# Routing of a token group in nine items instead of four, with the fourth group placed after the attention

## The reference

```python
x = x + _L2_xattn_ref(_layernorm(x, axis=-1), ctx_1024, ...)
def _L2_ffn_ref(x, ...):
    x = x + attention(layernorm(x, ln1_w), c_attn_w, c_proj_w)      # causal, 16 heads
    x = x + moe_mlp(layernorm(x, ln2_w), router_w, w1, w2)
def moe_mlp(x, router_w, w1, w2):
    probs = jax.nn.softmax(router_logits.astype(jnp.float32), axis=-1)
    rw, sel = jax.lax.top_k(probs, K)                               # K = 2 of E = 8
    h = jax.nn.gelu(jnp.einsum('nc,ecf->enf', xf, w1e), approximate=False)
    y = (y_sel * rw[:, :, None]).sum(axis=1)
```

## Time and profile before

| | |
|---|---|
| median of 3 runs | 3309.73 us (3307.66 to 3317.76) |
| profiled execution, its own time | 3314.98 us |
| its span | 3313.2 us |
| busy: PE, DVE, ACT, POOL | 85%, 60%, 50%, 34% of the span |
| granted TensorE clock, mean | 0.921 of full speed |

### The profile page before, as it was taken

How to read it: one execution, slowest core, us unless ns; L and a number is a source line. 1 busy time by engine, 2 the same in 40 slices (tenths; PEclk the granted TensorE clock), 3 DMA queues, 4 the chain that set the end, 5 groups by cost and what they waited for, 6 DMA issues and landing times. The chain is left out here.

```text
span 3313.2 us, 69870 instructions
## 1 busy us (share of the span) xinstructions
PE 2813.2 (85%) x25966; PEld 1896.0 (57%) x26085; DVE 1984.3 (60%) x4625; ACT 1663.2 (50%) x3058; POOL 1137.0 (34%) x1192
## 2 busy tenths in 40 slices
PE   4999686888789999999969999998469958999993
PEld 2554463555346666666635556666269936676672
DVE  4887555888455433433358887787554345555547
ACT  2778342777444444444427776766355513333332
POOL 6653008887000000000043334464400064565513
PEclk8999896999779999999969999999789968999995
DMA  3332002222214000000011211111243233332301
GB/s 115 74 74 60 14 5 90 66 67 68 45 53 147 1 1 1 1 1 1 1 60 58 74 47 51 41 61 56 81 143 97 84 100 79 81 83 63 77 20 51
DMA packets 164743, 189.87 MB, mean 57 GB/s; under 512 B 25968, under 2 KB 136832, under 8 KB 164256
## 3 DMA queue, kind: packets, MB, share of 16 engines
q1 hardware_dynamic: 147520, 143.44, 14.5%
q0 software_dynamic: 16896, 41.97, 4.9%
HBM read 67.09 MB, written 41.42 MB: 33 GB/s over the span
## 5 line engine op out<-in xcount | busy, mean ns | idle before, releaser
L1900 DVE TENSOR_TENSOR f1H<-f1HF,f1H 128x512 bf16<-128x512 f32 x256 | 176.6, 692 | 398.3 <-ACT f1H L1740 398.3
L1695 PE MATMUL ps<-f1w,f1H 128*128 128x256 bf16 x3072 | 379.1, 274 | 0.0
L1673 PE MATMUL ps<-f1xT,f1w 128*128 128x512 bf16 x1448 | 360.3, 384 | 12.1 <-ACT f1H L1740 5.9
L1695 PEld LDWEIGHTS ps<-f1w,f1H 128*128 128x128 bf16 x3072 | 301.8, 98 | 90.8 <-issue 1.7
L1737 ACT ACTIVATE f1HF<-ps 128x512 f32<-128x512 f32 x256 | 152.8, 597 | 333.9 <-PE ps L1673 333.8
L1061 ACT ACTIVATE a2PT<-ps 128x512 f32<-128x512 f32 (+1 forms) x512 | 260.1, 542 | 81.7 <-PE ps L884 58.7
L1673 PEld LDWEIGHTS ps<-f1xT,f1w 128*128 128x128 bf16 x1536 | 148.5, 99 | 152.5 <-issue 18.8
L861 PE MATMUL ps<-a2KS,a2QS 49*128 49x256 bf16 (+1 forms) x1024 | 175.9, 267 | 53.9 <-DVE a2NM L1196 20.9
L1583 POOL TENSOR_TENSOR f1RS<-f1VE,neghalf 128x4 f32<-128x4 f32 x8 | 8.1, 1011 | 578.0 <-DVE f1VE L1883 578.0
L1196 DVE TENSOR_REDUCE a0NM<-ps 128x2 f32<-128x512 f32 x256 | 165.5, 685 | 38.2 <-PE ps L861 37.6
L1196 DVE TENSOR_REDUCE a1NM<-ps 128x2 f32<-128x512 f32 x256 | 165.7, 686 | 37.5 <-PE ps L861 35.9
(11 more groups left out here) (538 smaller groups left out, 7046.0 us busy)
## 6 DMA issues: line engine op xcount, KB each, us to landing
a2KS<-a2KH SPq DMA_DIRECT2D x192, 64.0 KB
a2QS<-a2QH SPq DMA_DIRECT2D x192, 64.0 KB
a4KS<-a4KH SPq DMA_DIRECT2D x96, 128.0 KB
a4QS<-a4QH POOLq DMA_DIRECT2D x96, 128.0 KB, 4.3
slots<-zeros SPq DMA_DIRECT2D x1, 9984.0 KB, 31.9
f2XG<-slots SPq DMA_DIRECT2D x39, 256.0 KB, 2.9
results<-f2OB SPq DMA_DIRECT2D x39, 256.0 KB, 2.1
f1WF<-in_f_w SPq DMA_DIRECT2D x32, 256.0 KB, 2.7
```

What stands on the lines that cost most here:

```text
L1673: m = nc.tensor.matmul(ps[:, (u * NCH + i) % 2, :], w1[:, x, kt, i * P:i * P + P], xT[:, half, y, kt, :], start=(j == 0), stop=(j == len(t ...
L1695: m = nc.tensor.matmul(out, H[:, (u * NCH + i) % HR, x, t * P:t * P + P], w2[:, y, i, :], start=first, stop=(f == YC - 1 and j == 2 and no ...
L1900: nc.vector.tensor_tensor(H[:, (u * NCH + i) % HR, 1, :], HF[:, (u * NCH + i) % 2, :], H[:, (u * NCH + i) % HR, 0, :], SUB).then_inc(S["h_ ...
```

## The change

Four functions of `Router` become nine: `choose` is split into `compare`, `select` and `count`; `runs` into `need`, `first` and `jump`; `places` into `place` and `index`; `ranked` stays. The arithmetic is the same; two independent instructions in `first` swap places. In `slots()` they stand in the nine slots 1 to 9 of a period, where four stood in slots 1, 3, 5 and 7. Scatters move from slot 9 to slot 10. The new constant `PLACED` = 3 says that only groups 0 to 2 run their chain inside the list; `late` scatters units 8 to 11 two in a period (33 and 34). The chain of group 3 (units 12 and 13) moves into `routed`, ahead of the one of group 4, and the low halves of the weights are put between the steps of both chains. ACT takes its second, third and fourth high half in another order with the two `copied`.

```diff
-            put(1, "r_choose", "l", 0)
-            put(3, "r_rank", "l", 0)
-            put(5, "r_runs", "l", 0)
-            put(7, "r_places", "l", 0)
+            for k, n in enumerate(("r_compare", "r_select", "r_count", "r_rank", "r_need", "r_first", "r_jump", "r_place",
+                                   "r_index")):
+                put(1 + k, n, "l", 0)
...
-    return BATCH + b - 1 + 6 + u - a
+    return BATCH + b - 1 + 6 + (u - a) // (2 if n + 1 == PLACED else 1) if n < PLACED else None
...
-                        if r == "l" and v + 1 != GROUPS[n][1]:
+                        if r == "l" and (v + 1 != GROUPS[n][1] or n >= PLACED):
...
-                if router and k == 9:
+                if router and k == 10:
...
-                    if late(u) > 2 * BATCH + 3:
-                        router.scatter(pool, u)
+                for u in range(GROUPS[PLACED][0], BATCH):
+                    router.scatter(pool, u)
...
+                router.ranks(pe, PLACED, ps[:, 4, :])
...
-                for j in range(4):
-                    high(j)
-                for u in LATE:
-                    router.copied(act, u, ps[:, u % 2, :])
+                high(0)
+                high(1)
+                router.copied(act, INSIDE, ps[:, INSIDE % 2, :])
+                high(2)
+                high(3)
+                router.copied(act, INSIDE + 1, ps[:, (INSIDE + 1) % 2, :])
...
-                for u in LATE:
-                    router.stats(dve, u)
-                    router.negate(dve, u)
-                for u in LATE:
-                    router.kept(dve, u, ps[:, 2 + u % 2, :])
-                router.choose(dve, LAST)
+                router.stats(dve, INSIDE)
+                router.compare(dve, PLACED)
+                router.negate(dve, INSIDE)
+                router.stats(dve, INSIDE + 1)
+                router.select(dve, PLACED)
+                router.count(dve, PLACED)
+                router.negate(dve, INSIDE + 1)
+                router.ranked(dve, PLACED, ps[:, 4, :])
+                router.need(dve, PLACED)
+                router.first(dve, PLACED)
+                router.jump(dve, PLACED)
+                router.place(dve, PLACED)
+                router.index(dve, PLACED)
                 low(0)
+                router.kept(dve, INSIDE, ps[:, 2 + INSIDE % 2, :])
+                low(1)
+                router.kept(dve, INSIDE + 1, ps[:, 2 + (INSIDE + 1) % 2, :])
+                router.compare(dve, LAST)
+                router.select(dve, LAST)
+                router.count(dve, LAST)
+                low(2)
                 router.ranked(dve, LAST, ps[:, 5, :])
-                router.runs(dve, LAST)
-                router.places(dve, LAST)
+                router.need(dve, LAST)
+                router.first(dve, LAST)
+                router.jump(dve, LAST)
+                low(3)
+                router.place(dve, LAST)
+                router.index(dve, LAST)
+                low(4)
+                low(5)
                 table()
-                for j in range(1, len(PIECES)):
+                for j in range(6, len(PIECES)):
                     low(j)
```

More of the change, by code:

```diff
@@ L257, in ranked, with need, first @@
         self.nc.vector.tensor_copy(self.RR[:].rearrange("p t e -> p (t e)")[:, 0:c], bank[:, 0:c]).then_inc(S["r_rc"].sem, 1)
[L259 to L265, removed]
+    def need(self, dve, n):
+        nc, S = self.nc, self.S
+        total = self.RR[:, self.tiles(n)[1] - self.tiles(n)[0], :]
         dve.wait_ge(S["r_rc"].sem, S["r_rc"].at(n, 1))
-        self.link(dve, nc.vector.tensor_tensor(over, total, free, SUB))
-        self.link(dve, nc.vector.tensor_scalar(self.CI[:], over, 1.0, float(SLOT - 1), MUL, ADD))
+        self.link(dve, nc.vector.tensor_tensor(self.T[:, 0, :], total, self.FREE[:, n, :], SUB))
+        self.link(dve, nc.vector.tensor_scalar(self.CI[:], self.T[:, 0, :], 1.0, float(SLOT - 1), MUL, ADD))
         self.link(dve, nc.vector.tensor_scalar(self.CI[:], self.CI[:], 8, 0, ALU.arith_shift_right, ALU.logical_shift_left))
-        self.link(dve, nc.vector.tensor_copy(K, self.CI[:]))
+        self.link(dve, nc.vector.tensor_copy(self.T[:, 1, :], self.CI[:]))
+    def first(self, dve, n):
+        nc, E = self.nc, EXPERTS
+        over, K = self.T[:, 0, :], self.T[:, 1, :]
         self.link(dve, nc.vector.tensor_tensor(self.CT[:], self.T[:, 1:2, :].to_broadcast([P, E, E]),
@@ L279, in runs, with jump @@
+    def jump(self, dve, n):
+        nc = self.nc
+        total = self.RR[:, self.tiles(n)[1] - self.tiles(n)[0], :]
+        K, jump, add = (self.T[:, k, :] for k in (1, 2, 3))
+        self.link(dve, nc.vector.scalar_tensor_tensor(jump, self.FIRST[:, n, :], float(SLOT), self.FREE[:, n, :], MUL, SUB))
+        self.link(dve, nc.vector.tensor_tensor(jump, jump, self.BASE[:, n, :], SUB))
         self.link(dve, nc.vector.scalar_tensor_tensor(add, K, 0.0, jump, ALU.is_gt, MUL))
         self.link(dve, nc.vector.tensor_tensor(add, add, total, ADD))
[L281 removed]
@@ L1174, in _ @@
                         router.kept(dve, u, misc)
-                    elif name == "r_choose":
-                        router.choose(dve, i)
+                    elif name == "r_compare":
+                        router.compare(dve, i)
+                    elif name == "r_select":
+                        router.select(dve, i)
+                    elif name == "r_count":
+                        router.count(dve, i)
                     elif name == "r_rank":
                         router.ranked(dve, i, misc)
-                    elif name == "r_runs":
-                        router.runs(dve, i)
-                    elif name == "r_places":
-                        router.places(dve, i)
+                    elif name == "r_need":
+                        router.need(dve, i)
+                    elif name == "r_first":
+                        router.first(dve, i)
+                    elif name == "r_jump":
+                        router.jump(dve, i)
+                    elif name == "r_place":
+                        router.place(dve, i)
+                    elif name == "r_index":
+                        router.index(dve, i)
                     elif name == "sst" and u is not None:
```

53 lines of the change are left out of this document (31 added, 22 removed).

## The result

The changed kernel takes 3302.45 us (median of 12 executions, 3297.22 to 3308.79), the kernel before 3310.13 us in the same session (12 executions, 3305.16 to 3318.92). The ratio is 0.9974, 95% interval 0.9963 to 0.9984: 0.26% or 8 us faster, between the interval's ends 5 and 12 us. The forecast was 3297.2 us with a range of 3291 to 3305. The range holds the time, but the gain is two thirds of the 12.5 us forecast, and it is within the 0.3% that I called "same": the median stays above the line of 3299.8, which I had given 0.65 to be crossed.

The account below looks back on a forecast made before the run. Bounds: DVE in the periods of groups 0 and 1, POOL's routing scatters at the attention's end, late low halves in `routed`. From the median 3309.73 us, -6.8 - 5.7 + 0 = -12.5 gave 3297.2 us, range 3291 to 3305.

Parts of the forecast that it names:

- "same": Whole kernel: a time within 0.3% (9.9 us) of the kernel before, not to be told from no change; chance 0.30.
- the line of 3299.8: Whole kernel: the time in us below which the change counts as faster; chance 0.65.
- The start of `routed`: From the start of `routed` (T) to PE's first expert matmul: low halves between chain steps save 5.7 us, bounds 0 and -8.
- The hold by POOL's `split`: Start of `routed`: group 3's chain on DVE, held twice by POOL's `split`, delays the first low half 2 us; 0.5 taken off.
- The attention's end: POOL's last scatters ahead of `routed`: without waiting for a fourth group they end 6.8 us sooner, bounds -4 and -8.1.
- POOL still ends last: Attention's end: POOL's last scatter ends at 2363.6, DVE's last addition at 2361.0, 2.6 us ahead of it.
- The periods: Periods of groups 0 and 1 together: 0 change, between ends of -3.4 and +3.4 us.
- the rival of 30.2 us for each period: Periods of groups 0 and 1: later `f2SEL` costs clock, +3.4 us together, giving 3300.6 us; chance 0.15.
- DMA bandwidth: Weights in `routed`: last low half stays at T+51.3, only the attention's -6.8 us counts, giving 3302.9 us; chance 0.13.
- The attention's own end: Attention's end: ACT's late exponents slip over 2.6 us and become the bound; at 5 us, 3299.6 us; chance 0.05.
- The spread did not pay: Periods of groups 0 and 1: the rival judged said the spread pays in full, -3.4 us, giving 3293.8; chance 0.08.
- the clock did not stay low: Periods behind the chain periods: the rival judged had TensorE left at 1.2 GHz, up to 18.9 us per period, slower; chance 0.04.

Follow-up runs that it names:

- unit 9 between: The rank in slot 6 kernel with unit 9 scattered between `power` and `split` of unit 13 instead of ahead of `power`: ratio to the kernel before 0.9933.
- the changed kernel again: The changed kernel once more with no edit, against the kernel before: ratio 0.9982.
- the spread alone: Only the nine items in slots 1 to 9 and scatters in slot 10; group 3's routing and `routed` as in the kernel before: ratio to that 1.0018.
- Unit 11's move: Chains over two periods plus unit 9 between, with unit 11's four scatters moved from the attention's end into `routed`: ratio to the kernel before 0.9914.
- the second trace of the kernel before: The kernel before, unedited, traced again on another chip: periods of groups 0 and 1 28.58 and 27.79 us, no ratio given.
- the chains over two periods: Changed kernel, groups 0 and 1 with five items in one period, four in the next; group 2 as with the rank in slot 6: ratio to before 0.9936.
- four steps: The changed kernel without the spread, steps back in slots 1, 3, 5 and 7 and scatter in slot 9: ratio to the kernel before 0.9954.
- the rank in slot 6: The changed kernel with `rank` in slot 6 instead of 4, the five steps behind it in 7 to 11, scatter in 12: ratio to before 0.9952.
- slots 6 to 14: The changed kernel with groups 0 and 1's nine items in slots 6 to 14, their scatters behind the next unit's `split`: ratio to the kernel before 0.9962.
- the first session: One of three sessions on different chips; it ran the changed kernel again (0.9982), the spread alone (1.0018), four steps (0.9954) and the rank in slot 6 (0.9952).
- the low halves behind: Chains over two periods plus unit 9 between, with fifteen low halves put back behind group 4's chain and the table: ratio to the kernel before 0.9953.

## Why the prediction was right and where it failed

**The bounds** were read rightly: DVE in the chain periods, POOL at the attention's end, the ring of weights at the start of `routed`. The experiments moved the first by itself (the places of the steps) and the third (the low halves); the second was moved with unit 9 between and with unit 11, and together with the third in the changed kernel again against the spread alone.

**The start of `routed`, -5.7 forecast: -5.76 measured**, with the first low half (10 to 12: 11.95), the last one (T+45.1: T+45.55) and PE 1.1 us behind it. The hold by POOL's `split` was there: three small operations, L274, L287 and L295, took 0.57, 0.45 and 1.12 us instead of 0.17,

```profile
2377.47 0.57 DVE L274 TENSOR_TENSOR f2T<-f2RR,f2FREE 128x8 f32<-128x8 f32 x1
...
2379.47 0.45 DVE L287 SCALAR_TENSOR_TENSOR f2FREE<-f2T 128x8 f32<-128x8 f32 x1
...
2380.04 1.12 DVE L295 SCALAR_TENSOR_TENSOR f2T<-f2FIRST,f2FREE 128x8 f32<-128x8 f32 x1
```

together 1.6 us too much, where I had 2. L274 and L295 end with POOL's two subtractions. L287 ends at 2379.92 and POOL's cast (0.64 us from 2379.27) at 2379.91, so the cast holds DVE too, as the rule of the Trainium skill ("SBUF — State Buffer", "SBUF: two separate sides") has it; the loss stays small because the operations met each hold midway. Wrong, at no cost, was the forecast of the scatters: the last ended at T+38.3 instead of T+34.1. The first started at T+12.3 instead of T+10.1, and the sixteen took 26.0 us instead of the 20.0 that 1.27 us for each make: beside the low halves they took up to 2.35 us each (last section). SP issued `f2XG` at T+42.2 instead of T+38.5. Unit 11's move shows what this costs once it is the bound.

**The attention's end, -6.8 forecast: -2.6 measured against the trace on record.** The step that failed is "`negate` about 0.2, and ACT's `normalise` ... runs at 2350.7". In the changed kernel ACT starts it 2.6 us after the end of `power`, behind an evacuation and exponents that themselves wait for PE. I had the counterexample in hand: before, `power` ended at 2345.47 and `normalise` started at 2347.62, 2.15 us later. This is 2.3 us of the 4.2 missing; the first scatter of group 2, 1.7 us later relative to the last statistics than before, is most of the rest. Filling that wait with unit 9's scatters removed it. Nor is the handover a constant: it took 4.6 us in the second trace of the kernel before, 0.23 with the chains over two periods, where nothing was queued ahead of `normalise`, and 7.0 in the changed kernel again. The forecast that POOL still ends last held in the first trace (2367.51 against DVE's 2365.82), by 1.7 us, though DVE's addition came 5.1 us later than my walk had it, counted from the last statistics. In the changed kernel again, with four steps and with the rank in slot 6 it ended 0.7 to 2.1 us behind POOL's last scatter, and `routed` still started 4.25 us behind POOL.

How large the term is depends on the pair of traces. In the second trace of the kernel before the stretch takes 107.5 us instead of 104.5; against that the changed kernel's is 5.7 shorter, and the 101.1 of slots 6 to 14, on the same chip, 6.4. On the chip of the first session the two parts together brought 7.9 (the changed kernel again against the spread alone). So the -2.6 is the smallest of four readings, -6.8 lies within them, and one pair does not measure this term.

**The periods, 0 forecast: +3.9 measured.** "Ends for the two periods together: -3.4 and +3.4. I take 0, between them, nearest to the rows as they are" is the term that was mis-sized. The walk had the wait for `f2SEL` nearly right (4.3 us, measured 5.2). What it set against it is too small: "Behind `f2SEL` it then gets every further head after at most one item" was to take most of the 4.1 us of waits for maxima, and 2.3 stayed (in the second period 1.8 of 3.0). And a gain was left only if the clock fell less than before. It fell as much: 0.78 and 0.88 against 0.88 and 0.82. A longer stop at the same clock is the rival of 30.2 us for each period; measured 31.45 and 29.46, mean 30.5 (the first lies outside the 27 to 30 that I named as the sign). I gave this 0.15 and 3300.6 us; the median is 3302.45. The rival's name, "costs clock", is not what the two periods show, since PE's busy time over both is that of before: the price was the stop. The rule "nearest to the rows" failed: the rows of before contained no single stop of 5 us, and a spread that puts more DVE work ahead of `f2SEL` could not stay near them. That the four-step kernel, with the old waits, measures -15 us against a forecast of -12.5 without this term fits that, but its interval holds 12.5 as well.

The clock is what the better places gained in addition. Where no wait for `f2SEL` was left (rank in slot 6, two periods), every chain period but one was granted 1.00, and with the rank in slot 6 PE is busy 43.8 us over the two, against 47.1 with the nine items in slots 1 to 9 on that chip.

The length of the longest wait alone does not explain the clock. Before, it is 0.88 and 0.82 with a longest wait of 1.8 us, and in the changed kernel much the same with 5.2; yet it is 1.00 and 0.94 with unit 9 between, at 1.7. No run here separates what makes the difference.

**The range held partly by luck.** The two misses have one direction: +3.9 and +4.2 on 3297.2 give 3305.3, just outside 3291 to 3305. The median is lower because this pair of traces understates the gain: against the second trace of the kernel before, the same places sum to -6.8 us (+2.9, +0.2, +1.7, -5.7, -5.9), close to the timed 7.7, where against the first they sum to -4.6.

The rivals: DMA bandwidth did not set the weights (the last low half came 5.8 us sooner in the changed kernel, and 6.6 later again when the order alone was put back). The attention's own end did not become the bound, with the doubt named at unit 11's move. The spread did not pay, and the clock did not stay low behind the chain periods: the period behind group 0's takes 19.84 us at a clock of 1.00.

## What to carry to other kernels

Cutting a chain into pieces does not make room for it: what counts is what the other engine waits for out of the middle of the chain, and whether it has other work until then. Put the producer early, its consumer's turn later in the waiting engine's order, and look whether one period has the room at all; here 8.6 us had to be laid over two periods before they became cheap. Where a step is moved behind another, walk the queue of the engine that it is handed to: `normalise` started when ACT had got through what stood ahead of it, 0.23 to 7.0 us behind `power`, and not after the sum of the instructions in the handover. Two changes that fill the same engine's idle time overlap: measure them together before adding them. And an order that feeds a ring early (the low halves between the chain's pieces) gave its whole gain, at the size that a walk over the rows had given. Take a second trace of the kernel before, too: here it moved one term from -2.6 to -5.7 us.

## What the runs showed of the hardware that was not expected

A scatter, 0.96 us (now and then 1.05) and one per 1.27 us wherever it stands alone, takes up to 2.35 us beside DVE's low halves of 128x1024. POOL's timeline of the changed kernel in `routed`, and DVE's pair of low halves in the same microseconds:

```profile
2399.54 0.96 POOL L336 DMA_INDIRECT slots<-f2XS,IX  x1 [0.30 <-issue]
2400.81 2.35 POOL L336 DMA_INDIRECT slots<-f2XS,IX  x1 [0.30 <-issue]
2403.47 1.51 POOL L336 DMA_INDIRECT slots<-f2XS,IX  x1 [0.31 <-issue]
```

```profile
2399.86 2.46 DVE L2150 SCALAR_TENSOR_TENSOR f2w<-f2WF,f2GA,f2w 128x1024 bf16<-128x1024 f32 x2
```

The scatter of 2400.81 starts inside the pair and ends at 2403.16, 0.84 us behind the pair's end at 2402.32, nearly the 0.96 us of a whole scatter. The same 0.82 to 0.94 us lie between the end of a low half, or of a run of them, and the end of nearly every long scatter that starts within it, in the traces of the kernel before, of the changed kernel and its repetition, of unit 11's move and of the low halves behind: the longest are 4.49 us beside a run of four in the second trace of the kernel before, and 4.50 with the low halves behind. In the first trace of the kernel before, three scatters within such a run took 0.96 us all the same. So what counts is where a scatter starts, and a few more scatters beside such a stretch can cost more than their own sum.

On the chip of the first session ordinary periods beside which POOL scatters took 24.6 to 28.2 us, those without 19.7, in every kernel whose trace I have from there. In the repeated changed kernel DVE, ACT and PE all stand there for 3 to 4 us at once; DVE's timeline:

```profile
2196.43 0.62 DVE L1225 TENSOR_REDUCE a2NM<-ps 128x1 f32<-128x128 f32 x2 [0.48 <-PE ps L906]
2201.09 1.15 DVE L1225 TENSOR_REDUCE a2NM<-ps 128x1 f32<-128x128 f32 x4 [4.05 <-remote]
```

The row names no engine of this core for what ended the 4.05 us ("remote"). On the other chips the same periods take 19.7 to 20.1 us, in the kernel before and in the changed ones (but for one of 20.9 behind group 0's in slots 6 to 14). So the change alone does not bring it; no trace of the kernel before was taken on the first chip. What the engines wait for in it stays open. Both sides of a comparison carry it, but only roughly alike, which is a reason to trust the ratios of the first session least.
